# A chain of eight attention layers on one core: PSUM banks given out by a table, without filling products

## What is computed

```python
# a = 0, 1     16 heads of 8, length mask (a = 0 also causal)   a = 2  cross attention, then fc1/relu/fc2
# a = 3        causal self attention, 16 heads, after a feed-forward of 512 with a gate
# a = 4        cross attention on ctx, 16 heads                  a = 5, 6, 7   4 heads of 32, key and query masks
energy = einsum('bhst', Q, K) / sqrt(dk)          # + masks
score  = softmax(energy); out = einsum('bhsk', score, V)
x      = layer_norm(out + x) ...                  # eight times, each needs the one before
```

## Time and profile before

| | before |
|---|---|
| median of 3 runs | 1190.44 us |
| profiled execution | 1186.32 us |
| its span | 1184.4 us |
| PE busy | 1052.0 us, 89% |
| DVE busy | 870.4 us, 73% |
| ACT busy | 601.5 us, 51% |
| POOL busy | 220.9 us, 19% |
| mean granted TensorE clock | 0.974 |

### The profile page before, as it was taken

How to read it: one execution, slowest core, us unless ns; L and a number is a source line. 1 busy time by engine, 2 the same in 40 slices (tenths; PEclk the granted TensorE clock), 3 DMA queues, 4 the chain that set the end, 5 groups by cost and what they waited for, 6 DMA issues and landing times.

```text
span 1184.4 us, 37373 instructions
## 1 busy us (share of the span) xinstructions
PE 1052.0 (89%) x16224; PEld 761.2 (64%) x16351; DVE 870.4 (73%) x2508; ACT 601.5 (51%) x857; POOL 220.9 (19%) x320
## 2 busy tenths in 40 slices
PE   6869987989998999998989798869999989999895
PEld 4647655657767766665666576647676667766564
DVE  3688799965566655788896879997755765588886
ACT  4335444556656545554544353536756654654552
POOL 4001113210100111222320000231010010123333
PEclk9899999989999999999999998989999999999998
DMA  6001000000000000000000000000000000000001
GB/s 235 2 11 29 3 2 2 2 2 2 2 2 3 2 11 19 10 2 1 11 1 11 20 2 2 2 1 2 2 3 2 3 2 2 2 1 1 1 2 36
DMA packets 13715, 13.52 MB, mean 11 GB/s; under 512 B 617, under 2 KB 13170, under 8 KB 13298
## 3 DMA queue, kind: packets, MB, share of 16 engines
q1 hardware_dynamic: 13554, 11.14, 3.0%
HBM read 9.04 MB, written 2.10 MB: 9 GB/s over the span
## 4 chain that ended last, share of the span: by engine, by line
PE 48%; DVE 38%; ACT 5%; POOL 4%; issue 4%; DMA 0%; SPq 0%; POOLq 0%; DVEq 0%; ACTq 0%
DVE mx L1257 9%; PE bank L857 9%; PE bank L665 9%; PE bank L889 9%; PE bank L732 5%; PE bank L863 5%; PE bank L652 4%; DVE stats L999 4%; DVE X L1023 4%; PE bank L765 3%; ACT PT L932 2%; DVE Y L1009 2%; DVE Y L1017 2%; DVE Y L1061 2%; DVE mv L1002 2%
## 5 line engine op out<-in xcount | busy, mean ns | idle before, releaser
L932 ACT ACTIVATE PT<-bank 128x1024 f32<-128x1024 f32 x184 | 185.0, 1025 | 220.6 <-PE bank L863 181.4
L1257 DVE TENSOR_REDUCE mx<-bank 128x16 f32<-128x1024 f32 x184 | 217.9, 1216 | 34.4 <-PE bank L863 25.9
L857 PE MATMUL bank<-KQ 32*128 32x128 f32 (+3 forms) x4416 | 194.8, 267 | 46.2 <-DVE mx L1257 16.9
L857 PEld LDWEIGHTS bank<-KQ 32*128 32x128 f32 (+3 forms) x4416 | 159.8, 161 | 108.7 <-DVE mx L1257 31.5
L889 PEld LDWEIGHTS bank<-V,PT 128*64 128x64 f32 x5888 | 185.7, 139 | 54.2 <-issue 37.7
L889 PE MATMUL bank<-V,PT 128*64 128x32 f32 (+2 forms) x5888 | 202.4, 225 | 8.4 <-DVE Y L1061 4.1
L665 PE MATMUL bank<-xf,W_all 128*128 128x512 f32 x336 | 180.0, 633 | 6.1 <-ACT xf L903 3.5
L1283 POOL TENSOR_SCALAR ve<-mv 128x4 f32<-128x4 f32 x64 | 15.6, 243 | 675.8 <-DVE mv L1002 662.7
L903 ACT ACTIVATE KQ<-bank,c 128x512 f32<-128x512 f32 x160 | 100.6, 687 | 69.5 <-PE bank L665 68.9
L903 ACT ACTIVATE V<-bank 64x512 f32<-64x512 f32 x128 | 79.2, 619 | 43.9 <-PE bank L765 42.0
L1052 DVE RECIPROCAL rd<-bank 128x32 f32<-128x32 f32 (+1 forms) x128 | 37.6, 294 | 73.2 <-PE bank L889 72.6
(11 more groups left out here) (112 smaller groups left out, 1593.3 us busy)
## 6 DMA issues: line engine op xcount, KB each, us to landing
W_all<-weights SPq DMA_DIRECT2D x1, 2880.0 KB, 12.4
Xin<-x SPq DMA_DIRECT2D x8, 256.0 KB, 3.0
C<-ctx SPq DMA_DIRECT2D x8, 256.0 KB, 4.0
out<-X SPq DMA_DIRECT2D x8, 256.0 KB, 2.3
row<-rows SPq DMA_DIRECT2D x1, 1024.0 KB, 6.0
c<-const SPq DMA_DIRECT2D x1, 536.0 KB, 5.9
W_all<-weights SPq DMA_DIRECT2D x1, 192.0 KB, 3.2
c<-const SPq DMA_DIRECT2D x1, 80.5 KB, 2.0
```

The lines of the kernel that those rows point to most:

```text
L857: last[u] = pe.matmul(banked[u // 2][:, at:at + 2 * S], stationary[rows_, seq].rearrange("p r t -> p (r t)"), moving[rows_, seq].rearrange ...
L932: act.activation(PT[:, n % NPT, :], banks.of("B", a, s, v)[:], ACT.Exp, scale=float((D // (2 * PAIRS[a])) ** -0.5)).then_inc(*banks.drain( ...
L1257: dve.tensor_reduce(dst, banks.of("A", a, s, v)[:].rearrange("p (u m t) -> p u m t", u=2, t=S), AX.X, ALU.max).then_inc(*banks.drain(("A", ...
```

## The change

Banks are now eight equal ones in four tensors `pair0` to `pair3`, and each step on PE names the bank that it takes in the table: `A0@01` takes pair 0 for its first half and pair 1 for its second, `v2@6` takes bank 6. The counting of places is in units of the width, so scores use places 0 and 1 of width 2 (banks 0 to 3), as before. Everything else, outputs among it, uses banks 4 to 7: 124, 178, 216 and 266 times. In attentions 5 to 7, where a score step needs one pair alone, the table names which (0 in 36 cases, 1 in 12) instead of taking turns. `v1` and `v3` name none, since they write on where `v0` and `v2` began. `take` waits as before for the readers of what stood last in each bank.

```diff
-    def claim(self, due, ring, *use):
-
-        n = self.turn[ring] = self.turn.get(ring, -1) + 1
-        k = ring[n % len(ring)]
-        if self.section.known and k in self.last:
-            for sem, count in self.section.known["readers"][self.last[k]].items():
-                due[sem] = max(due.get(sem, 0), count)
-        self.last[k] = use + (self.section.group,)
+    def claim(self, due, k, width, *use):
+
+        use += (self.section.group,)
+        for bank in range(k, k + width):
+            if self.section.known and bank in self.last:
+                for sem, count in self.section.known["readers"][self.last[bank]].items():
+                    due[sem] = max(due.get(sem, 0), count)
+            self.last[bank] = use
...
-BANKS = (1024, 1024, 512, 512, 512, 512)
 OUT, WIDE, FILL = 160, 32, 512
-RING_S = (0, 1)
-RING_O = (2,)
-RING_M = (3, 4, 5)
...
                 def step(name, a, s):
-                    if "+" in name:
-                        name, n = name.split("+")
+                    name, _, n = name.partition("+")
+                    name, _, where = name.partition("@")
+                    places[:] = map(int, where)
+                    if n:
...
-                        outputs[0] = room(RING_O, "O", a, s, half)
+                        outputs[0] = room("O", a, s, half)
...
+                g_.memset(warm[:], 1.0).then_inc(*pool.mark("warm"))
```

No step carries a `+n` any more: the 295 filling products are gone, with their weight loads. (`fill` would now use a tile `warm` that POOL sets; nothing calls it.) The table was written anew for all engines. It has the same steps, and a step stands on PE 0.9 places from where it stood in the mean, 7 at most; on DVE 0.8, on ACT 0.7. Two lines of PE's table, before and after:

```diff
-        0.0.0 x+1; 0.0.1 x; 0.0.2 x; 0.0.0 pq pk pv; 0.0.1 pq; 0.0.0 first; 0.0.1 pk; 0.0.0 length; 0.0.1 pv+1; 0.0.0
+        0.0.0 x@7 pq@7; 0.0.1 x@6; 0.0.2 x@5; 0.0.0 pk@4 pv@7 first@5; 0.0.1 pq@4 pk@5; 0.0.0 length@4; 0.0.1 pv@7;
```

More of the change, by code:

```diff
@@ L58 @@
[L58 to L62, removed]
@@ L68 @@
[L68 to L72, removed]
@@ L83 @@
[L83 to L86, removed]
-        pk pv; 0.5.1 maxrow; 0.5.0 v1; 0.5.3 q; 0.5.1 B0; 0.5.2 ksum+1; 0.5.1 v0+3; 0.5.3 up0; 0.5.2 maskrow; 0.5.3
@@ L378, in __init__, with view, take @@
     def __init__(self, ctx, nc, section):
-        self.filled = [ctx.enter_context(nc.semaphore(f"filled{k}")) for k in range(len(BANKS))]
-        self.tensor = [ctx.enter_context(nc.psum_tensor(f"bank{k}", [P, w], F32)) for k, w in enumerate(BANKS)]
-        self.section, self.uses, self.last, self.turn = section, [0] * len(BANKS), {}, {}
+        self.filled = [ctx.enter_context(nc.semaphore(f"filled{k}")) for k in range(8)]
+        self.pairs = [ctx.enter_context(nc.psum_tensor(f"pair{k}", [P, 1024], F32)) for k in range(4)]
+        self.section, self.uses, self.last = section, [0] * 8, {}
         self.readers = section.counts["readers"]
-    def take(self, pe, ring, *uses):
+    def view(self, k, width):
+        at = 512 * (k % 2)
+        return self.pairs[k // 2][:, at:at + 512 * width]
+    def take(self, pe, places, width, *uses):
         due = {}
-        taken = [self.claim(due, ring, *use) for use in uses]
+        taken = [self.claim(due, width * place, width, *use) for place, use in zip(places, uses, strict=True)]
         for sem, count in due.items():
@@ L408, in of @@
     def of(self, *use):
-        return self.tensor[self.section.known["filled"][use + (self.section.group,)][0] if self.section.known else 0]
+        return self.view(*(self.section.known["filled"][use + (self.section.group,)][:2] if self.section.known else (0, 2)))
     def ready(self, *use, ago=0):
@@ L634, in _, with fill, room @@
             def _(pe):
-                held = {}
-                def fill(ring, n, *use):
-                    loaded(c16_in)
-                    held[use], = banks.take(pe, ring, use)
+                held, places = {}, []
+                def fill(n, width, *use):
+                    loaded(pool, "warm")
+                    held[use], = banks.take(pe, places[:1], width, use)
                     for _ in range(n):
-                        pe.matmul(held[use][:, 0:FILL], K16("identb"), c16[:, 0:FILL], start=True, stop=True)
-                def room(ring, *use):
-                    return held.pop(use) if use in held else banks.take(pe, ring, use)[0]
+                        pe.matmul(held[use][:, 0:FILL], warm[:], warm[:].unsqueeze(1).broadcast_to((P, FILL // 128, 128)),
+                                  start=True, stop=True)
+                def room(*use):
+                    return held.pop(use) if use in held else banks.take(pe, places, 1, use)[0]
                 def turn(src, use):
-                    t = room(RING_M, *use)
+                    t = room(*use)
                     for j in range(NT):
@@ L844, in score_banks @@
                     early = [held.pop(use) for use in uses if use in held]
-                    return early + banks.take(pe, RING_S, *uses[len(early):])
+                    return early + banks.take(pe, places[len(early):], 2, *uses[len(early):])
                 def scores(kind, a, s, half, stationary, moving, banked):
```

483 lines of the change are left out of this document (256 added, 227 removed).

## The result

The changed kernel took 1197.5 us as the median of 18 runs (1193.9 to 1204.3), against 1192.8 us for 18 runs of the kernel before. The ratio is 1.0052 with a 95% interval of 1.0030 to 1.0074: about 6 us slower, where 17.5 us faster was forecast. The time lies outside the forecast's own range (1160 to 1182) and inside the range for 8 in 10 (1150 to 1201), near its slow end, and it moved the other way than forecast.

A forecast was written before the change was run, and what follows sets the result against it. Neither PE nor DVE alone was taken as the bound, but a chain changing hands between them. Terms -3.5 - 12 - 8 - 9 + 7 + 8 = -17.5 us gave 1173 us; own range 1160 to 1182, 8 in 10 from 1150 to 1201.

The forecast's parts named there:

- The clock: PE without filling products: 31 us more at the low clock, costing 8 us (bounds 0 and 34 us).
- The filling products: PE's 295 extra products, used to fill its waits: removing them saves 12 us (bounds 0 and 34).
- PE's idle time would grow by less than 60 us: Sign for removing the filling products: PE busy time down about 66 us, idle time up by less than 60.
- The order: Values steps moved behind turns' waits for norms on PE: 15 times 0.64 us, taken as 9 us saved (bounds -4 to 19).
- The banks: Outputs and other steps sharing four single banks: 8 of 9.8 us of PE's bank waits saved (bounds 0 to 20).
- Its sign: Sign for shared banks: PE's values steps wait under 2 us for DVE's division.
- The start: First turn on PE near 4.3 us, first Qf before 14 us, `first` 2 to 4.3 us earlier: 3.5 us saved.
- Issue: PE's sequencer: 188 more waiting instructions at 0.041 us each, costing 7 us (bounds 0 and 8).
- The clock decides: Rival: PE falls to the low clock in thin stretches; break-even at 98 us more low time; 1210 us; chance 0.18.
- signs of failure: Prediction wrong if the clock is under 0.93 or idle time before scores grows by as much as the filling products.
- nothing moves: Rival: DVE and score pairs hold the chain; PE's savings become waits for the maxima; 1189 us; chance 0.27.
- the same: Outcome class: measured time within about 1% of before, neither faster (under 1178.5 us) nor slower; chance 0.31.

The follow-up runs named there:

- e1: Kernel before with its 295 filling products taken out, nothing else changed: 1202.4 us, 1.0103 of before.
- e4: Kernel before, same order, with outputs and other steps sharing four single banks by a table, and without filling products: 1193.4 us, 1.0025 of before.
- e8: Changed kernel with each step given the single bank whose readers were done first in its trace: 1196.4 us, 1.0032 of before.
- e5: e4 with 548 filling products at 148 places where PE stood still in e4's trace: 1172.5 us, 0.9843 of before.
- e7: Changed kernel with 518 filling products at 140 places where PE stood still in its own trace: 1184.2 us, 0.9915 of before.
- e11: Kernel before, same order and banks, its old filling products replaced by 519 in 154 waits of e1's trace: 1178.7 us, 0.9887 of before.
- e3: Kernel before, same order and filling products, with outputs and other steps sharing four single banks by a table: 1186.2 us, 0.9985 of before.

## Why the prediction was wrong, step by step

**The sum by edits.** The runs without products for the clock lead from one kernel to the other, one edit at a time (1% is 11.9 us):

| edit | runs | measured | forecast |
|---|---|---|---|
| filling products out, with clock and issue | before to e1 | +12.3 us | -12 + 8 + 7 = +3 |
| banks shared | e1 to e4 | -9.3 | -8 |
| start and order | e4 to e8 | +0.8 | -3.5 - 9 = -12.5 |
| the table's choice of banks | e8 to after | +2.4 | none, taken as ideal |
| sum | | +6.2 | -17.5 |

Each of these has an interval of some 4 to 7 us to either side, and the runs come from two chips. The step of the banks agrees. The two that failed are the first by 9 us and the order by 13 us; the 2 us of the choice of banks are within their interval here. The row of start and order also holds the choice of score pairs.

**The clock.** This term was mis-sized. The price was about right: over 29 runs of the kernel before, each us at the low clock goes with 0.33 us of time, over 18 runs of after with 0.24 us, and the forecast had 0.26 (the other kernels, with 4 to 22 runs each, give 0.21 to 0.43). The amount was wrong: 31 us more at the low clock was forecast. It is 67 us between the two profiled executions, and 47 us between medians (128 and 81), because the profiled execution of before, from which the 62 us were read, was at the fast end of its runs (clock 0.974, those 29 from 0.956 to 0.973). 47 us at 0.24 to 0.33 are 11 to 16 us instead of 8. With the filling products alone removed (e1) it is 79 us over those 29 runs, and 87 over before's runs on e1's own chip. The forecast took their share of PE's busy time, 6%, and half again of the low time by feel; it should have looked at where they stood, which was in the stretches with gaps. The Trainium skill (TensorE: Matmul & The Clock Gate, "HAM oscillation — how this bites in real kernels") tells of an engine that falls back to the slow clock in the waits between its bursts and starts each burst slow; e1, with 79 us more at the low clock, and e5 and e7, with 117 and 95 us less once the waits were filled, agree with its direction. The forecast's upper bound of 130 us more was not reached.

The dips were also read at the wrong places of the row: they stand in slices 2, 9, 25, 27 and 40, not 7, 19, 26 and 28. The windows beside it (240 to 280 and 760 to 800 us) were read rightly, and no term hung on the slices.

**The filling products** cost time of their own as forecast. At 0.24 to 0.33 us per us of low clock (the slopes above), 79 to 87 us more low time in e1 are 19 to 29 us (an estimate). e1 is 12.3 us slower, so some 7 to 17 us were saved, with the issue's cost already in it and e1's own interval of 5 us on top. The 12 us read from the chain's pieces fit, but are not confirmed closely. That PE's idle time would grow by less than 60 us held: its idle time, the span less the busy time, grew from 132 to 160 us.

**The order.** The reading was right and the conclusion wrong. Turns do wait less for norms (4.0 us for X L1041, and the 8.6 us for L1009 are 3.0), and nothing came of it. The 0.64 us in front of the turn was counted as a gain, the delay of what is moved back was not; the term took one place and multiplied it by 15, for a table that was written anew throughout. It put -9 us where start and order together measured +0.8. The bound of +4 for "a table that is new everywhere" may have been too small: near full clock the order costs 3 us with the start's 4.5 us of gain in it, so some 7 us by itself, give or take 6. Which of the moved steps costs it stays open.

**The banks.** Sharing gave 9 us without products (e1 to e4), 5 with products in the waits (e11 to e5) and 2 with the old ones (before to e3), each give or take some 5, so the forecast's 8 is not refuted. Its sign, waits for the division under 2 us in the kernel after, was missed: 3.1. And the forecast took any table for a good one. After's uses bank 7 in 266 steps and bank 4 in 124, and waits for single banks rose from 28.3 to 34.1 us instead of vanishing; with even use (198, 202, 195, 189) they are 24.8 us in the same order.

**The start** was about right: the first turn at 4.09 us (4.3 forecast), `first` 1.9 us earlier (2 to 4.3 forecast), 2.4 and 3.5 us at the first values steps of streams 0 and 1, 4.5 us in the mean with the clock held. Qf came at 14.38 us, not before 14; the last section shows why. Without filling products only 1.3 us of it was left in the mean at the end of attention 0; the clock's fall at 35 us is the likely cause, since the gain stays where the clock is held.

**Issue.** The chain's share of issue went from 42.7 to 49.5 us, 6.8 us against the 7 forecast. That is partly luck: e1, which has 894 of these waiting instructions on PE, 186 more than before and 2 fewer than after, shows 46.7 us, 4.0 more, and between e3 and e4 the same removal goes with 1.2 us more.

**The rivals.** "The clock decides" was the right mechanism, with losses by the new order named in it; its break-even of 98 us more low time was not reached, and the sum turned all the same, since it had kept the 9 us of the order as a gain. Of the signs of failure named ahead, the clock (0.946) stayed above 0.93, and the idle time before scores grew by 23 us, a third of the filling products. Neither gave the warning; the waits of scores for maxima and the exponential, which rose from 31 to 50 us, did. That rise is what "nothing moves" described: what PE saves turns into waits for the maxima. By the forecast's own measure, about 1% to tell a change, the outcome is "the same", to which it gave 0.31, though with a larger clock term and a losing order in it.

## What to carry to other kernels

A product that nobody reads is good where the array would stand still and bad one step further on: the same kind of products cost 1.6% at places taken over from another order and gave 1.4% at the waits of their own trace. So after any change of order, take them out, profile, and place them anew; whether a second placing gains more was not told apart here. And price a moved step by what now waits behind it as well as by the wait that it fills (that this sum would have come out right wasn't tried); compare clocks over many runs before reading a small difference.

## What the hardware showed that was not expected

DVE's mask operation on 128x4 takes 0.17 us in most places, and 1.94 us here (timeline of after; both POOL and DVE):

```profile
7.42 0.17 DVE L1057 TENSOR_SCALAR qm<-am 128x4 f32<-128x4 f32 x1
...
11.27 1.98 POOL L1290 MEMSET V<- 128x1152 f32 x2
11.33 1.94 DVE L1057 TENSOR_SCALAR qm<-am 128x4 f32<-128x4 f32 x1
...
14.38 0.22 DVE L1226 TENSOR_TENSOR Qf<-KQ,c 128x64 f32<-128x64 f32 x1
```

I had taken it for a slow first one; but after's first took 0.17 us, at 7.42. It ends at 13.27 us, when POOL's two memsets end (13.25). In the kernel before it starts at 11.20 and ends at 13.08, the memsets at 13.05; in e3 it starts at 11.69 and takes 1.52 us, to 13.21, the memsets to 13.19. So it isn't slow, it stands until POOL is done, on the path to the first Qf. The other traces say the same: in all 13 it starts between 10.86 and 11.69 us, takes 1.42 to 2.36 us and ends within 0.03 us of the memsets. In e8 it also caught the COPY behind the first mask (`m<-qm`), which took 2.40 us from 7.81 to 10.21 us, with two memsets to 10.18; and the reduction `am<-Xin`, which overlaps a memset in several traces, kept its 0.69 us. The Trainium skill (SBUF — State Buffer, "SBUF: two separate sides") says of the ports that VectorE and GpSimd share that they are "an exclusive lock, not a bandwidth split": of a GpSimd instruction and a VectorE one in a mode that uses both ports, the one that starts first keeps them for its whole length. The traces agree that DVE stands still rather than slows down, but they don't show the mode, and here DVE stood through two memsets in a row. Whether moving the memsets elsewhere would free some 1.7 us at the start (an estimate: 1.94 less 0.17) wasn't tried.

The clock fell in one place after waits that were short one by one (at 35.0 us in after; the longest in the ten us before was 0.57 us, and PE was busy in 9.2 of them), so a view of the longest waits doesn't always foretell it. And products of 16 columns, at the same places and as many, held it little better than none (0.944 against 0.934, with 0.966 at 512 columns).
